# Softmax row sums of an attention block: from PSUM by ScalarE, or copied by VectorE first; three probability buffers for two

## The reference, cut to what matters

```
xn = layernorm(x)
Q, K, V = heads of 64 out of xn @ W
scores = Q K^T / sqrt(64)            # layer 1: causal
attn = softmax(scores)               # exp(scores) / sum of exp(scores) over the keys
out = (attn @ V) @ Wo
x = x + out * silu(ffn(xn))
```

## Time and profile before

| | us |
|---|---|
| Runs of the kernel before | 4937.98 and 5144.42, median 5041.2 |
| Profiled execution, its own time | 4935.12 |
| Profiled execution, span of its slowest core (core 3) | 4933.5 |
| Spans of the eight cores | 4904.2 to 4933.5 |
| PE, DVE, ACT busy on core 3 | 3664.4, 1286.7, 1328.4 |

### The profile page before, as it was taken

The page is one execution under the profiler, slowest core; times in us unless marked ns, Lnnn a source line. Parts: engine busy times, 40 slices in busy tenths (PEclk is TensorE's granted clock), DMA queues, the critical chain, the costliest instruction groups (busy, mean ns, idle before and its releaser), DMA issues.

```text
span 4933.5 us, 44326 instructions; the slowest of 8 cores (4904.2 to 4933.5 us)
## 1 busy us (share of the span) xinstructions
PE 3664.4 (74%) x14712; PEld 1452.0 (29%) x14712; DVE 1286.7 (26%) x2076; ACT 1328.4 (27%) x1573; POOL 282.2 (6%) x522
## 2 busy tenths in 40 slices
PE   2246667899999999976777777743999966666675
PEld 0012222344444444432222222211444422222221
DVE  3332320033033023122222222224101023443332
ACT  1100000011011011004666565611111101445563
POOL 1000000000000000000000000010101000000000
PEclk9878888899999999988898989865999999889998
DMA  2257778744434434330011111144444320122121
GB/s 75 62 145 205 198 193 195 177 143 145 154 128 138 153 137 145 137 92 9 13 37 32 37 32 37 28 100 98 73 74 77 69 47 8 33 41 58 35 50 45
DMA packets 139086, 450.92 MB, mean 91 GB/s; under 512 B 15568, under 2 KB 15728, under 8 KB 122480
## 3 DMA queue, kind: packets, MB, share of 16 engines
q0 software_dynamic: 73632, 218.42, 21.6%
q1 hardware_dynamic: 65232, 229.67, 13.6%
HBM read 490.23 MB, written 73.40 MB: 114 GB/s over the span
## 4 chain that ended last, share of the span: by engine, by line
PE 53%; DMA 16%; DVE 15%; ACT 10%; issue 5%; DVEq 1%; SPq 0%; ACTq 0%; POOL 0%; POOLq 0%
ACT a16t L1488 9%; PE pst L745 8%; PE pst L759 8%; PE pst L861 4%; PE pb L861 4%; DMA a32t<-l_u 4%; PE pb L1002 3%; PE pb L1437 3%; PE pst L938 3%; PE pst L949 3%; DMA a16t<-s_g 3%; PE pst L1460 2%; PE pst L1354 2%; PE pst L1465 2%; PE pb L1442 2%
## 5 line engine op out<-in xcount | busy, mean ns | idle before, releaser
L1488 ACT ACTIVATE a16t<-pst 128x1024 bf16<-128x1024 f32 x832 | 851.7, 1024 | 607.0 <-PE pst L1465 534.1
L745 PE MATMUL pst<-xn_sb,a16t 128*128 128x512 bf16 x2304 | 600.0, 407 | 183.9 <-DVE a16t L693 157.7
L759 PE MATMUL pst<-xn_sb,a16t 128*128 128x512 bf16 x2304 | 567.2, 391 | 0.0
L1437 PE MATMUL pb<-a16t 128*65 128x512 bf16 x832 | 342.4, 412 | 288.6 <-DVE a16t L1576 118.7
L772 ACT ACTIVATE a32t<-pst 128x512 f32<-128x512 f32 x288 | 172.0, 597 | 1113.4 <-PE pst L745 1113.4
L1460 PE MATMUL pst<-a16t 128*128 128x512 bf16 x832 | 350.3, 421 | 163.0 <-DVE a16t L1399 103.8
L780 DVE TENSOR_TENSOR a32t<-a32t,pst 128x512 f32<-128x512 f32 x256 | 176.1, 688 | 1130.3 <-PE pst L759 1130.3
L745 PEld LDWEIGHTS pst<-xn_sb,a16t 128*128 128x128 bf16 x2304 | 227.3, 102 | 503.2 <-issue 284.6
L1465 PE MATMUL pst<-a16t 128*128 128x512 bf16 x832 | 349.7, 420 | 0.0
L1442 PE MATMUL pb<-a16t 128*65 128x512 bf16 x832 | 342.4, 412 | 0.0
L759 PEld LDWEIGHTS pst<-xn_sb,a16t 128*128 128x128 bf16 x2304 | 233.0, 101 | 298.6 <-issue 47.4
(11 more groups left out here) (156 smaller groups left out, 2744.6 us busy)
## 6 DMA issues: line engine op xcount, KB each, us to landing
a16t<-s_g POOLq DMA_DIRECT2D x108, 512.0 KB, 5.0
a16t<-s_u SPq DMA_DIRECT2D x108, 512.0 KB, 3.4
a32t<-l_u SPq DMA_DIRECT2D x32, 1024.0 KB, 10.8
a16t<-s_d SPq DMA_DIRECT2D x27, 1024.0 KB, 5.0
a16t<-s_d POOLq DMA_DIRECT2D x27, 1024.0 KB, 5.5
s_g<-a16t SPq DMA_DIRECT2D x36, 512.0 KB, 7.3
s_u<-a16t SPq DMA_DIRECT2D x36, 512.0 KB, 8.2
s_d<-a16t SPq DMA_DIRECT2D x18, 1024.0 KB, 8.4
```

What stands on the lines that cost most here:

```text
L745: li = t.matmul(pb[gp_][:, :], a16t[:, o_gb[wp] + hc * 256 + ici * 128: o_gb[wp] + hc * 256 + ici * 128 + 128], xn_sb[:, hc * T + tc * TC: ...
L759: li = t.matmul(pb[up_][:, :], a16t[:, o_ub[wp] + hc * 256 + ici * 128: o_ub[wp] + hc * 256 + ici * 128 + 128], xn_sb[:, hc * T + tc * TC: ...
L1437: t.matmul(pb4[0:65, :], a16t[:, o_vtm + kc * 65 * nvh + kva * 65: o_vtm + kc * 65 * nvh + kva * 65 + 65], a16t[:, o_pt[kp]:o_pt[kp] + TC] ...
L1488: return s.activation(a16t[:, o_pt[kp]:o_pt[kp] + 2 * TC], pst[kp][:, 0:1024], AF.Exp, scale=0.125)
```

## The change

Four things are different, all in `phase_C`.

1. The probabilities get three buffers: `o_pt` has three entries and is indexed by `kc % 3` (`kp4`). The scores still have two PSUM tiles.
2. `o_nrm` is no longer allocated but lies at the fixed place `A16 - 1024`.
3. A new VectorE operation `f_sums`, listed after `f_oevb`, copies the row sums from partition 64 of `pb4` and of `pb5` to `o_sums` in SBUF: two 1x512 copies. It waits for the last product and for the `f_rcp` of the block before.
4. `f_rcp` takes one logarithm of all 1024 sums from SBUF instead of two of 512 from PSUM; the exponential is the same. It now waits for `f_sums`, where it waited for the last product. The broadcast waits for `f_rcp` as before.

```diff
-            o_pt = [a16.alloc(2 * TC) for _ in range(2)]
+            o_pt = [a16.alloc(2 * TC) for _ in range(3)]
...
-            o_nrm = a16.alloc(2 * TC)
+            o_nrm = A16 - 1024
...
-                        def f_exp(s, kc=kc, kp=kp):
+                        kp4 = kc % 3
+
+                        def f_exp(s, kc=kc, kp=kp, kp4=kp4):
                             return s.activation(
-                                a16t[:, o_pt[kp]:o_pt[kp] + 2 * TC],
+                                a16t[:, o_pt[kp4]:o_pt[kp4] + 2 * TC],
                                 pst[kp][:, 0:1024], AF.Exp, scale=0.125)
-                        de = [op_st, pv.get(("avpt", kp))]
+                        de = [op_st, pv.get(("avpt", kp4))]
...
+                        def f_sums(v):
+                            v.tensor_copy(a32t[0:1, o_sums:o_sums + TC],
+                                          pb4[64:65, :])
+                            v.drain()
+                            return v.tensor_copy(
+                                a32t[0:1, o_sums + TC:o_sums + 2 * TC],
+                                pb5[64:65, :])
+                        op_sums = P.add("V", f_sums,
+                                        deps=[op_avl, pv.get(("rcpd",))],
+                                        name=f"C{L}sums{qc}.{p}")
+
                         def f_rcp(s):
-                            s.activation(a32t[0:1, o_rcf:o_rcf + TC],
-                                         pb4[64:65, :], AF.Ln)
-                            s.drain()
-                            s.activation(a32t[0:1, o_rcf + TC:o_rcf + 2 * TC],
-                                         pb5[64:65, :], AF.Ln)
+                            s.activation(a32t[0:1, o_rcf:o_rcf + 2 * TC],
+                                         a32t[0:1, o_sums:o_sums + 2 * TC], AF.Ln)
                             s.drain()
                             return s.activation(a16t[0:1, o_nrm:o_nrm + 2 * TC],
                                                 a32t[0:1, o_rcf:o_rcf + 2 * TC],
                                                 AF.Exp, scale=-1.0)
-                        op_rcp = P.add("S", f_rcp, deps=[op_avl, pv.get(("bcd",))],
+                        op_rcp = P.add("S", f_rcp, deps=[op_sums, pv.get(("bcd",))],
                                        name=f"C{L}rcp{qc}.{p}")
-                        op_sums = op_rcp
+                        pv[("rcpd",)] = op_rcp
```

More of the change, by code:

```diff
@@ L1432, in emit_av, with f_av @@
                     def emit_av(kc, kva=kva, kvb=kvb, nkc=nkc, qc=qc, p=p):
-                        kp = kc % 2
+                        kp4 = kc % 3
                         pt_d = exp_ops[kc][1]
-                        def f_av(t, kc=kc, kp=kp, kva=kva, kvb=kvb, nkc=nkc):
+                        def f_av(t, kc=kc, kp4=kp4, kva=kva, kvb=kvb, nkc=nkc):
                             t.matmul(pb4[0:65, :],
@@ L1439, in f_av @@
                                           o_vtm + kc * 65 * nvh + kva * 65 + 65],
-                                     a16t[:, o_pt[kp]:o_pt[kp] + TC],
+                                     a16t[:, o_pt[kp4]:o_pt[kp4] + TC],
                                      start=(kc == 0), stop=(kc == nkc - 1))
@@ L1445, in f_av @@
                                      o_vtm + kc * 65 * nvh + kvb * 65 + 65],
-                                a16t[:, o_pt[kp] + TC:o_pt[kp] + 2 * TC],
+                                a16t[:, o_pt[kp4] + TC:o_pt[kp4] + 2 * TC],
                                 start=(kc == 0), stop=(kc == nkc - 1))
@@ L1451, in emit_av @@
                         op = P.add("T", f_av, deps=dav, name=f"C{L}av{qc}.{p}.{kc}")
-                        pv[("avpt", kp)] = op
+                        pv[("avpt", kp4)] = op
                         return op
@@ L1497, in phase_C, with f_msk @@
                             j = kc - 4 * qc
-                            def f_msk(v, kp=kp, j=j):
-                                v.tensor_tensor(a16t[:, o_pt[kp]:o_pt[kp] + TC],
-                                                a16t[:, o_pt[kp]:o_pt[kp] + TC],
+                            def f_msk(v, kp4=kp4, j=j):
+                                v.tensor_tensor(a16t[:, o_pt[kp4]:o_pt[kp4] + TC],
+                                                a16t[:, o_pt[kp4]:o_pt[kp4] + TC],
                                                 a16t[:, o_cm + j * TC:
```

## The result

The changed kernel takes 5225.5 us (median), against 4936.8 us for the kernel before on the same chip. The ratio is 1.057, 95% interval [1.055, 1.060]. The forecast was 5210 us, +5.6%, in a range of 5130 to 5330.

What follows compares the result with a forecast made beforehand. ScalarE's exponentials bound the steady part, a separate chain the block ends. Longer chain 245 us plus TensorE clock 30, buffers 0, make 275 us on 4935: 5210 us, +5.6%, range 5130 to 5330.

Steps and rivals of the forecast that it cites:

- What bounds it: Steady part bound by ScalarE's exponentials, 1.17 us start to start; between blocks, a separate chain from L1532 to the next product.
- Three buffers: 0 us: Third probability buffer gains nothing: exponentials also wait for their scores, which TensorE's order puts behind the product freeing the buffer.
- The price of one copy: Each new 1x512 row-sum copy on VectorE: 0.68 us, between 415 ns (L360) and 0.69 us (L1532).
- The block ends: Copies and reciprocal come onto the path at 64 block ends: 83 + 31 + 67 + 26 + 32 + 6 = 245 us.
- the plain end of layer 0: 22 of layer 0's 31 ends: broadcast, normalization and next first product come 3.75 us later each, 83 us.
- the ends with a fusion: 8 layer 1 ends where a 1.5 us VectorE fusion stood before L1568: lose 3.2 us each, 26 us.
- those with a mask: 7 layer 1 ends where chunk 0's mask stands between L1532 and L1568: lose 4.6 us each, 32 us.
- The clock: TensorE idles longer at block ends; 18 blocks lose full clock at 1.8 us each: 30 us taken, bounds 0 to 80.
- Faster by the third buffer: Rival: the buffer removes 0.15 us between exponentials, 125 us, giving 4810 us with the epilogue hidden; 2%.
- Still hidden: Rival: the longer reciprocal stays covered at the block ends, no change, 4935 us; 3%.
- The clock pays much more: Rival: TensorE regains 2.4 GHz later, all 62 ends pay 1.8 us more, 112 us: 5322 us; 10%.
- the mark that I had set: Sign against the prediction: PEclk of layer 0's attention, 0.88 before, falling below about 0.8 or rising.

Runs made afterwards that it cites:

- idle matmuls: Changed kernel plus 8 matmuls whose results nobody reads, between the next block's first scores and the broadcast, where no output projection is under way: 1.058 [1.049, 1.067].
- the fastest kernel: Kernel before with the epilogue's copies and reciprocal listed at the block's end, broadcast and normalization ahead of the next scores: 0.9735; with 10 unread matmuls at 16 ends, 0.967.
- the kernel with the whole epilogue early: Kernel before with copies and reciprocal listed at the block's own end, broadcast and normalization ahead of the next block's first scores: 0.970, then 0.9735 when measured again.
- the wait alone: Kernel before with one added dependency: the reciprocal also waits for the copy of the second product, L1532; no instruction added: 1.037 [1.024, 1.050].

## Why the prediction was right, point by point

*What bounds it.* Right. The steady part stayed as it was: the exponential is 1.024 us and the mean of its idle time changed only because the waits at the block ends went elsewhere. The block end is a chain of its own, and what was added to it came out in the total: a third copy of 0.76 us made each end of layer 0 0.75 us longer.

*Three buffers: 0 us.* Right, 1.0005 alone.

*The price of one copy.* 0.68 us from the nearest row, L425; 0.685 us measured, at 1 partition and from PSUM. The logarithm of 1024 was taken at 1.055 us and is 1.055. The lower bound by L360 (415 ns, out of SBUF) was not near. The Trainium skill ("VectorE: DVE Perf Modes", "Why PSUM operands drop a tier") says that an operand in PSUM keeps an fp32 copy at the basic rate; the two rows, 685 and 415 ns, agree.

*The block ends.* The list of kinds of ends held: 3.75 us was forecast for the plain end of layer 0, and the mean from the end of the second product's copy to the next product, over all 31, rose by 3.83 (forecast (83 + 31) / 31 = 3.68). In layer 1 the ends with a fusion lose 3.25 to 3.4 (forecast 3.2), those with a mask 4.4 to 4.9 (4.6), the full-clock plain ones 4.35 (4.3), the last ends 2.9 and 3.0 (3.0). The sum over all 64 was forecast as 245 us, and is 119 + 127 + 6 = 252 by this measure, from the copy's end (the table above has 4 us less for layer 1, since it includes the query matmuls, some of which met another clock). Of the 7 us missing, 5 are in layer 0 and 2 in layer 1. About 2 us are one gap: between L1534 and L1540 it is 0.17 us at 31 ends of layer 0, not the 0.11 that I took from the pair L1568, L1576; that is the gap of a VectorE operation that also waits for another engine, as after L1399 in the last timeline. In layer 1 it is 0.10. The others are spread over the ends: six of layer 0 had taken 2.89 us and not 3.02, and lose 3.99; the nine with a projection matmul lose 3.6 on average and not 3.45.

*The shape of the rest of the chain.* The fusion does disappear under the reciprocal, and the mask does come behind the exponential, which is behind the reciprocal. Both were worked out from the order on the engines alone.

*The clock: the term that was mis-sized.* Forecast 30 us, measured 43 on core 3 (24 in layer 0, 19 in layer 1), and 27 to 50 by core, 39 on average. The step "if all of these lose it, that is 18 x 1.8 = 32" held for the blocks that it counts: all of them lost the full clock at their start, and on core 3 they lost 18.3 us (ten in layer 0) and 15.5 us (eight in layer 1), 34 in all. What it left out is the other blocks, which it let pay nothing: some with two slow chunks came to have three, for 0.5 to 1 us, and they add up to 9 us. The bounds (0 to 80) held it. The idle matmuls show it as the clock in layer 0 only.

*The total.* The sum gave 275 us more, and the timed runs took 289 more. The 274 us between the two spans of core 3 are nearer to it by luck: its attention lost 292, and 18 were made up ahead of it, where nothing was changed.

*The rivals.* Faster by the third buffer: excluded. Still hidden: excluded, with 64 waits on the reciprocal and 255 us of idle TensorE. The clock pays much more: no, 43 us and not 142, and on no core more than 50; on core 3 the granted clock in layer 0's attention is 0.80, just at the mark that I had set at "about 0.8". What I had not seen as a rival is how much of the cost is not in the copies: two thirds of the longer ends (158 of 241 us) come from the wait by itself.

## What to carry to other kernels

Work on an engine with idle time is free only at certain places in its order: before handing it to another engine, look at what is queued there ahead of it, since on engines that work in order a new wait carries all of that onto its path. Here two copies of 0.69 us cost almost 4 us at each block end, because a reciprocal that had run beside the next block's queries came to stand behind them. The other way round it pays too: the epilogue listed where its inputs are ready, not where its result is needed, made this kernel 2.7% faster than before (0.9735) with the same instructions in another order.

## What the runs showed of the hardware that I had not expected

- Idle matmuls can pay for themselves: in layer 0 a stretch with 152 more of them was 22.6 us shorter, at a granted clock of 0.85 instead of 0.81, and in the fastest kernel 160 took the ratio from 0.9735 to 0.967.
- A copy of 512 elements out of PSUM took VectorE as long for one partition as for 64: 685 ns for the 1x512 copy L1540 and 684 for the 64x512 copy L1534. Two rows of sums cost as much as the two whole products.
- The gap between two operations on VectorE, a semaphore wait apart, is 0.10 us where the second waits for its own engine alone (L1534 behind L1527), and 0.17 us where it waits for another as well (L1540 behind L1534 in layer 0, L1568 behind L1399 in the kernel with the whole epilogue early), although that other one had long been done. In layer 1 VectorE has already waited for a later value of ScalarE's semaphore, for a mask, when it comes to L1540; no second wait is issued, and the gap is 0.10.
- Short idle stretches of TensorE cost the clock at some block ends and not at others. Idle for 3.2 us ahead of the scores and 1.7 us ahead of the first product, TensorE began 9 to 11 of 31 blocks in layer 0 at full clock (1.00, or 2.4 GHz); with a third stretch between them, of 2.3 us (the wait alone) or 3.7 us (the changed kernel), it began none.
